# Three gated layers' last products in two-part float16, on one core of a Trainium2 chip

## The chip, the cores and the metric

The kernel runs on 1 NeuronCore of one Trainium2 chip. The number that counts is the device time of one execution in microseconds (us). The kernel before takes 786.88 us (median of 3 runs, 783.63 to 787.39). Engines are called as the profile calls them: PE is TensorE's matmul, PEld its weight load, DVE is VectorE, ACT is ScalarE, POOL is GpSimd, SP is SyncE.

## The reference, cut to what matters

Input is x of shape (2, 1024, 128); six layers are applied to it, each to the layer norm of x, each added back.

```python
x = x + 0.5 * int8_ffn(_layernorm(x))            # layer 0
x = x + attention_16_heads_of_8(_layernorm(x))   # layer 1, causal
x = x + 0.5 * int8_ffn(_layernorm(x))            # layer 2
x = x + 0.5 * gated_ffn(_layernorm(x))           # layer 3
x = x + attention_16_heads_of_64(_layernorm(x))  # layer 4, causal
x = x + 0.5 * gated_ffn(_layernorm(x))           # layer 5

def gated_ffn(x):                  # weights are integers in -127..127, times 1/127
    gate = x @ wg.T                # 128 -> 384
    up = x @ wu.T                  # 128 -> 384
    h = silu(gate) * up
    return h @ wd.T                # 384 -> 128
```

The gated layer is run four times: layer 3 and layer 5, each for batch 0 and batch 1. The change is about the last product, h @ wd.T, of three of the four.

## The kernel before, in words

Everything of one batch (1024 rows, 128 columns) is 8 tiles of 128 rows. A start section does the first layers of batch 0 by hand-written code. Then comes one list of 985 steps, `PLAN`, made from a string of letters, `ORDER`: each letter takes the next step of its own stream. Small letters are the attention of layer 1 in 8 groups of 4 heads (`m` maxima, `t` turning them, `e` exponentials, `w` weighing the values, `g` and `a` around them); capital letters are the attention of layer 4 in 16 pairs of heads (`Q`, `K`, `V` projections, `M` maxima, `T` turning them, `E` exponentials, `W` weighing, `S` sums, `O` output projection); `h` is the string of all the other layers, which depend on one another in order. Below, the stretch of the small letters is called the group stage and that of the capitals the pair stage. Every engine walks the same `PLAN` in the same order and does its part of each step, so a step that waits holds back all later steps on its engine. Behind the list a closing section finishes the last pair and runs layer 5 of batch 1 by hand-written code.

PE writes its products into PSUM. Steps that fill PSUM take banks in turn, two at a time for most (`deal_banks`), and PE waits until the readers of the earlier user of these banks are done (`wait_for_banks`). So some three such steps are under way at once.

A gated layer in the list is: the norm (`ln`, `xt`), six `up` steps (3 chunks of 128 hidden columns, 2 halves of 512 rows) and one `down` step. In an `up` step PE makes gate and up (float16 products, L1376), ACT takes the tanh of the gate (L808), and DVE makes h from them with two instructions (L1061, L1062), which go to `ffn_h` in float32. In the `down` step PE multiplies `ffn_h` by `wd_s`, 8 tiles by 3 chunks (24 matmuls in float32, L1382), and DVE adds the result to x (L1042).

POOL works in three roles here. In the start section it converts the weights of the gated layer (L570, L571) between other work (L580, L575) of the first attention. In the list it does most of the layer norms, the integer layer's rounding, and in the pair stage seven additions for each pair of heads: the exponentials of a chunk are added into a running sum (L679), 128x1024 elements each; and one multiplication (L525). ACT may not overwrite a chunk's buffer before PE has weighed it and POOL has added it; there are six such buffers.

A `T` step goes PE (L1444), ACT (L838), DVE (L1113), then two small DMAs on SP's queue into the tile that the first `E` step of the pair reads.

## Time and profile before

| | |
|---|---|
| median of 3 runs | 786.88 us (783.63 to 787.39) |
| the profiled execution's own time | 787.15 us |
| its span, first to last instruction | 785.4 us |
| busy over the span | PE 92%, PEld 55%, DVE 68%, ACT 58%, POOL 59% |
| mean granted PE clock | 0.963 of full |

The difference of 1.75 us between the profiled execution's time and its span lies before the first and behind the last instruction that the profile counts. Busy PE means that at least one matmul is in flight, so 92% is not 92% of PE's peak. An idle engine costs nothing unless the engine that sets the pace waits for it. The profile's rows stand in a section of their own below.

### The profile page before, as it was taken

To read this page: it belongs to the slowest core of one execution; us is meant where nothing else is said; L and a number is where in the kernel's file an instruction comes from. 1 tells how busy PE (TensorE), PEld (TensorE's weight loads), DVE (VectorE), ACT (ScalarE), POOL (GpSimd) and SP (SyncE) were. 2 spreads that over 40 slices of the span, in tenths; PEclk is the share of its full clock that TensorE was granted. 3 is DMA by queue.
4 is the path that set the end of the run, shared out by engine and by line. 5 is a ranking of instruction groups with operands and counts; after the bars stand their busy time and mean duration, and the time that the engine had idled before them with its cause. 6 is when DMAs were issued, how large, how long until landed. Compare 5 with 4: busy or idle time off the path is not lost.

```text
span 785.4 us, 21560 instructions
## 1 busy us (share of the span) xinstructions
PE 718.6 (92%) x9387; PEld 428.2 (55%) x9387; DVE 532.5 (68%) x730; ACT 454.4 (58%) x535; POOL 467.1 (59%) x367
## 2 busy tenths in 40 slices
PE   3667988889888899999999999999999999999997
PEld 1433535345344454655555566645776655557764
DVE  7599888998878785778587645665645655643037
ACT  2425876987776679554746546556544565563502
POOL 6814546522841210499989759978457967689630
PEclk9955998999889999999999999999999999999999
DMA  8000000000000000001001101110110110112100
...
DMA packets 13226, 16.20 MB, mean 21 GB/s; under 512 B 3053, under 2 KB 10573, under 8 KB 13133
## 3 DMA queue, kind: packets, MB, share of 16 engines
...
q8 instruction: 75, 1.23, 0.7%
...
## 4 chain that ended last, share of the span: by engine, by line
PE 74%; DVE 11%; ACT 9%; issue 3%; POOL 1%; DMA 1%; SPq 0%; ACTq 0%; DVEq 0%; POOLq 0%
PE ps L1261 20%; PE ps L1210 17%; ACT Pr L697 7%; DVE big L1074 7%; PE ps L1181 6%; PE ps L1425 5%; PE ps L1240 5%; PE ps L1464 3%; PE ps L1432 3%; PE ps L1382 2%; PE ps L1271 2%; PE ps L1376 2%; PE ps L1251 1%; PE ps L1221 1%; PE ps L1231 1%
## 5 line engine op out<-in xcount | busy, mean ns | idle before, releaser
L697 ACT ACTIVATE Pr<-ps,exp_scale 128x1024 f32<-128x1024 f32 (+1 forms) x294 | 278.8, 1006 | 122.2 <-PE ps L1261 74.1
L679 POOL TENSOR_TENSOR V0s<-V0s,Pr 128x1024 f32<-128x1024 f32 x77 | 181.4, 2356 | 106.4 <-PE ps L1210 60.6
L1105 DVE TENSOR_REDUCE mxb<-ps 128x8 f32<-128x1024 f32 (+1 forms) x152 | 173.6, 1163 | 86.0 <-PE ps L1261 66.5
L1074 DVE TENSOR_REDUCE big<-ps 128x8 f32<-128x1024 f32 (+1 forms) x159 | 170.2, 1116 | 22.7 <-PE ps L1240 16.0
L1261 PE MATMUL ps<-big 64*128 64x128 f16 (+2 forms) x2560 | 168.3, 259 | 0.9 <-DMA big<-turns 0.7
L1240 PE MATMUL ps<-big 32*128 32x128 f16 (+2 forms) x1280 | 105.1, 280 | 32.9 <-DVE big L1074 15.6
L1261 PEld LDWEIGHTS ps<-big 64*128 64x128 f16 x2560 | 92.8, 94 | 71.0 <-issue 23.9
L1210 PE MATMUL ps<-Pr,V1s 128*64 128x128 f32 (+2 forms) x960 | 110.2, 370 | 0.0
L1240 PEld LDWEIGHTS ps<-big 32*128 32x128 f16 x1280 | 42.5, 95 | 108.8 <-ACT Pr L697 44.0
L679 POOL TENSOR_TENSOR acts<-acts,Pr 128x1024 f32<-128x1024 f32 x35 | 82.4, 2355 | 22.3 <-PE ps L1210 12.4
L1210 PEld LDWEIGHTS ps<-Pr,V1s 128*64 128x64 f32 x960 | 57.0, 136 | 41.4 <-issue 28.2
L1181 PE MATMUL ps<-Pr,V0s 128*18 128x128 f32 (+2 forms) x1280 | 79.4, 373 | 0.2 <-ACT Pr L704 0.2
L1099 DVE TENSOR_TENSOR big<-ps,big 128x1024 f16<-128x1024 f32 (+1 forms) x33 | 39.0, 1191 | 30.3 <-ACT big L697 29.7
L1261 PE MATMUL ps<-big,shr_s 64*128 64x256 f16 (+2 forms) x384 | 55.8, 287 | 0.0
L1425 PE MATMUL ps<-XT,wqkv 128*128 128x512 f16 x192 | 45.2, 380 | 0.1
L697 ACT ACTIVATE big<-ps 128x1024 f16<-128x1024 f32 (+1 forms) x33 | 32.7, 997 | 19.8 <-PE ps L1425 19.7
L1181 PEld LDWEIGHTS ps<-Pr,V0s 128*18 128x18 f32 x1280 | 30.4, 100 | 18.8 <-issue 11.0
L594 POOL TENSOR_TENSOR stats<-moments 128x8 f32<-128x8 f32 x9 | 1.9, 210 | 63.1 <-DVE moments L1018 63.1
L525 POOL TENSOR_TENSOR big<-Pr,rec_b 128x1024 f32<-128x1024 f32 x15 | 36.5, 2431 | 3.7 <-DMA rec_b<-scratch_dram 2.5
L691 ACT ACTIVATE big<-ps 128x512 f32<-128x512 f32 (+2 forms) x31 | 19.3, 622 | 33.0 <-PE ps L1394 17.9
L697 ACT ACTIVATE V0s<-ps,exp_scale 128x1024 f32<-128x1024 f32 x22 | 24.5, 1114 | 19.1 <-PE ps L1251 17.8
L1425 PEld LDWEIGHTS ps<-XT,wqkv 128*128 128x128 f16 x192 | 17.4, 98 | 21.3 <-issue 2.1
...
## 6 DMA issues: line engine op xcount, KB each, us to landing
...
```

Source lines behind the costliest of these rows:

```text
L525: g.tensor_tensor(YT[:, p % NP], y_raw[p % 2], rec_b[:], ALU.mult).then_inc(normed, 1)
L679: g.tensor_tensor(dst, dst, src, ALU.add).then_inc(summed, 1)
L697: ins = a.activation(dst[:, part], src, func, scale=scale)
L1074: ins = v.tensor_reduce(maxima_of(mall[:, r, 2 * u:2 * u + 2][:, part], i), block_view(src, i), AX.X, ALU.max, negate=True)
L1099: ins = v.tensor_tensor(in_banks(low)[:, part], src, in_banks(high)[:, part], ALU.subtract)
L1105: ins = v.tensor_reduce(maxima_of(mxb[:, r][:, part], arg), block_view(src, arg), AX.X, ALU.max, negate=True)
L1181: ins = te.matmul(ps[HR * j:HR * j + 2 * VW, ACC0, a0 - 512 * half:a1 - 512 * half], values(g // GB, t, GH * (g % GB) + j, half), src, sta ...
L1210: ins = te.matmul(ps[h * D1:(h + 1) * D1, ACC1[bank], a0 - 512 * bank:a1 - 512 * bank], V1[p % SETS][:, t, h * D1:(h + 1) * D1], src, star ...
L1240: ins = te.matmul(slot[h][:, off:off + a1 - a0], still[rows, tile(t)], moving[rows, a0:a1], start=q == 0, stop=cut is None and q == len(pi ...
L1261: ins = te.matmul(slot[h][:, off:off + a1 - a0], still[rows], moving[rows], start=q == 0 and k == 0, stop=not goes_on and q == len(pieces) ...
L1425: ins = te.matmul(slot[half], w16[:, ww], x16[:, xx, half_of(half)], start=part == 0, stop=part == 2)
L1432: ins = te.matmul(tile_of(slot, t), x16[:, xx, tile(t)], w16[:, ww], start=part == 0 and t % 4 == 0, stop=part == 2, skip_group_check=True)
```

## The change

Three of the four gated layers are touched: layer 3 of both batches, and layer 5 of batch 0, the ones in the list. Layer 5 of batch 1, in the closing section, keeps its float32 product.

- A new kind of step, `split`, stands behind each `up` step, six in a layer. DVE now writes h of an `up` step into one of three buffers (`ffn_t`, float32). In the `split` step ACT copies it to float16 (the high part), and POOL subtracts the high part from h and writes the remainder in float16 (the low part). DVE waits before it writes a buffer again until POOL has read it.
- `down` multiplies both parts by a float16 copy of the integer weights (`wd_16`), 8 tiles by 3 chunks by 2 parts: 48 matmuls in float16 in place of 24 in float32.
- The up weights, and with them h, are scaled by 2^-14 (`H_SCALE`); the scale factors behind are set for it. In the start section POOL's one conversion of gate and up weights becomes two instructions, and the copy to `wd_16` is added at the end of POOL's start work.
- `ORDER` is another string: 1003 steps in place of 985, with all letters placed anew.
- The program's scratch for dynamic DMA is set to 1024.

```diff
 def gated_steps(s, b):
-    return (turned_norm_steps(s, b) + [("up", (s, b), (c, half), "AV") for c in range(HC) for half in range(2)]
-            + [("down", (s, b), None, "V")])
+    ups = [[("up", (s, b), (c, half), "AV"), ("split", (s, b), 2 * c + half, "")] for c in range(HC) for half in range(2)]
+    woven = ups[0][:1] + [step for k in range(1, len(ups)) for step in (ups[k][0], ups[k - 1][1])] + ups[-1][1:]
+    return turned_norm_steps(s, b) + woven + [("down", (s, b), None, "V")]
...
-    "ammmmmmmmammmmmmmmmmamtmmehemehmhmemememmmweehmwemmwemwemewemehwmehewemhthweaemehweemwegemehwmemwemm"
+    "ammmmmmmmammmmmmmmmmamtmmmeeehemmhhememmmwmhewemewemewemhwmemwememehemwthweahemeweehmwegemehwmemwmem"
...
+        ffn_t = sb("ffn_t", [P, TERMS, 512])
+        ffn_16 = ffn_h[:, :, :].rearrange("p c s -> p (c s)").bitcast(F16).rearrange("p (w c s) -> p w c s", w=2, c=HC)
...
             pool.wait_ge(raw_in, 16 * R_LOADS)
-            g.tensor_copy(wg_s[:], raw_gu)
+            g.tensor_copy(wg_s[:, 0], raw_gu[:, 0])
+            g.tensor_scalar(wg_s[:, 1], raw_gu[:, 1], H_SCALE, None, ALU.mult)
             g.tensor_scalar(wd_s[:], raw_d, W_SCALE, None, ALU.mult).then_inc(converted, 1)
...
+            g.tensor_copy(wd_16[:], raw_d).then_inc(converted, 1)
...
+                if kind == "split":
+                    c, half = divmod(arg, 2)
+                    pool.wait_ge(h_high, SPLIT_NO[key, arg] + 1)
+                    g.tensor_tensor(ffn_16[:, 1, c, half_of(half)], ffn_t[:, arg % TERMS], ffn_16[:, 0, c, half_of(half)],
+                                    ALU.subtract).then_inc(h_low, 1)
...
+                if kind == "split":
+                    c, half = divmod(arg, 2)
+                    act.wait_ge(slot_dve, read("V", "up", key, (c, half)))
+                    a.activation(ffn_16[:, 0, c, half_of(half)], ffn_t[:, arg % TERMS], ACT.Copy).then_inc(h_high, 1)
...
-                    v.tensor_tensor(ffn_h[:, c, 512 * half:512 * half + 512], gate, slot[1],
-                                    ALU.mult).then_inc(slot_dve, 1)
+                    if 2 * c + half >= TERMS:
+                        dve.wait_ge(h_low, SPLIT_NO[key, 2 * c + half - TERMS] + 1)
+                    v.tensor_tensor(ffn_t[:, (2 * c + half) % TERMS], gate, slot[1], ALU.mult).then_inc(slot_dve, 1)
...
                 if kind == "down":
-                    pe.wait_ge(slot_dve, read("V", "up", key, (HC - 1, 1)))
+                    pe.wait_ge(h_low, SPLIT_NO[key, GATED - 1] + 1)
+                    pe.wait_ge(converted, 2)
                     for t in range(T):
                         for h in range(HC):
-                            ins = te.matmul(tile_of(slot, t), ffn_h[:, h, tile(t)], wd_s[:, h], start=h == 0,
-                                            stop=h == HC - 1)
+                            for w in range(2):
+                                ins = te.matmul(tile_of(slot, t), ffn_16[:, w, h, tile(t)], wd_16[:, h],
+                                                start=(h, w) == (0, 0), stop=(h, w) == (HC - 1, 1))
...
-    nc = bacc.Bacc("TRN2", target_bir_lowering=False, num_devices=1)
+    nc = bacc.Bacc("TRN2", target_bir_lowering=False, num_devices=1, dynamic_dma_scratch_size=1024)
```

What the new code and the new string do to the engines' instructions is shown at three places. In the first, POOL in the start section, before and after; `wg_s` and `wd_s` are the converted weights, `V1s` and `big` belong to the first attention's keys and queries.

```order
L568 MEMSET big 128x512
L570 CAST wg_s<-Pr 128x768
L571 TENSOR_SCALAR wd_s<-Pr 128x384
L580 TENSOR_TENSOR big<-V1s,big 128x8x8x8
L575 TENSOR_TENSOR V1s<-V1s,big 128x1024
```

```order
L578 MEMSET big 128x512
L580 CAST wg_s<-Pr 128x384
L581 TENSOR_SCALAR wg_s<-Pr 128x384
L582 TENSOR_SCALAR wd_s<-Pr 128x384
L591 TENSOR_TENSOR big<-V1s,big 128x8x8x8
L586 TENSOR_TENSOR V1s<-V1s,big 128x1024
```

One TENSOR_SCALAR more stands ahead of the first subtraction for keys and queries (L580 before, L591 after).

The second place is POOL after the change, during layer 3 of batch 1 in the pair stage. L696 are the additions of exponentials (L679 before), L535 the multiplication (L525 before), L675 the new subtractions of the `split` steps.

```order
L696 TENSOR_TENSOR acts<-acts,Pr 128x2x512
L675 TENSOR_TENSOR ffn_h<-ffn_t,ffn_h 128x512
L696 TENSOR_TENSOR acts<-acts,Pr 128x8x128
L696 TENSOR_TENSOR acts<-acts,Pr 128x2x512
L535 TENSOR_TENSOR big<-Pr,rec_b 128x1024
L696 TENSOR_TENSOR V0s<-V0s,Pr 128x2x512
L696 TENSOR_TENSOR V0s<-V0s,Pr 128x4x256
L696 TENSOR_TENSOR V0s<-V0s,Pr 128x2x512
L675 TENSOR_TENSOR ffn_h<-ffn_t,ffn_h 128x512
L696 TENSOR_TENSOR V0s<-V0s,Pr 128x4x256
```

The subtractions stand one by one between the additions; before, nothing of the gated layer's products stood on POOL.

The third place is PE at the last `down` step of the list (layer 5, batch 0), before and after. L1382 and L1407 are `down`, L1444 and L1469 the `T` step of the last pair, L1432 its `V` step, L1210 and L1233 `W` steps, L1261 and L1284 (128x128 x24) the first of its `E` steps.

```order
L1221 MATMUL ps<-pick_s,cutq_s 128x4x64 x4
L1382 MATMUL ps<-wd_s,ffn_h 128x128 x24
L1444 MATMUL ps<-id_s,mxc 16x128
L1432 MATMUL ps<-wqkv,XT 128x128 x24
L1210 MATMUL ps<-Pr,V1s 64x512 x2
L1210 MATMUL ps<-Pr,V1s 64x128 x16
L1261 MATMUL ps<-big 128x128 x24
```

```order
L1244 MATMUL ps<-pick_s,cutq_s 128x4x64 x4
L1233 MATMUL ps<-Pr,V1s 64x256 x4
L1233 MATMUL ps<-Pr,V1s 64x512 x2
L1233 MATMUL ps<-Pr,V1s 64x128 x8
L1469 MATMUL ps<-id_s,mxc 16x128
L1407 MATMUL ps<-wd,ffn_h 128x128 x48
L1233 MATMUL ps<-Pr,V1s 64x128 x8
L1284 MATMUL ps<-big 128x128 x24
```

Before, `down` stood ahead of the `T` step, and the `V` step and three `W` steps between `T` and `E`; now `down` and one `W` step stand between them.

## Rows read from the trace of the kernel before

**Rows 1.** Windows of the four stages: us; busy of each engine (instructions); PEclk, DMA.
```profile
0.00:34.80 34.80, 15.51 (x93) 10.42 (x93) 24.94 (x65) 9.03 (x21) 25.50 (x58) 1.00 0.48 156
34.80:321.40 286.60, 246.76 (x3639) 131.68 (x3639) 237.75 (x319) 206.60 (x250) 102.44 (x116) 0.90 0.01 2
321.40:742.00 420.60, 419.71 (x5366) 259.35 (x5365) 248.48 (x290) 232.37 (x258) 328.73 (x190) 1.00 0.08 21
742.00:785.40 43.40, 36.67 (x295) 26.76 (x294) 21.32 (x57) 6.37 (x11) 10.39 (x5) 1.00 0.09 25
```

**Rows 2.** Page, section 2: PE's granted clock in 40 slices, tenths of full.
```profile
PEclk9955998999889999999999999999999999999999
```

**Rows 3.** Timeline, first `down`: start, us, engine, line, out<-in, count, [idle before <-releaser].
```profile
256.73 5.43 PEld L1382 LDWEIGHTS ps<-wd_s,ffn_h 128*128 128x128 f32 x48 [0.23 <-issue]
...
262.40 1.23 DVE L1042 SCALAR_TENSOR_TENSOR X<-ps,X 128x1024 f32<-128x1024 f32 x1 [3.49 <-PE ps L1382]
...
262.78 3.28 ACT L697 ACTIVATE Pr<-ps,exp_scale 128x512 f32<-128x512 f32 x4 [5.93 <-PE ps L1240]
```

**Rows 4.** Timeline, one `V` step's weight loads.
```profile
318.74 1.34 PEld L1432 LDWEIGHTS ps<-wqkv,XT 128*128 128x128 f16 x24
```

**Rows 5.** Groups by form: count, busy us, mean ns, idle before and releasers.
```profile
L1382 PEld LDWEIGHTS ps<-wd_s,ffn_h 128*128 128x128 f32 x144 | 16.3, 192 | 0.9 <-issue 0.9
L1062 DVE TENSOR_TENSOR ffn_h<-ffn_g,ps 128x512 f32<-128x512 f32 x18 | 12.4, 687 | 0.6
L1061 DVE SCALAR_TENSOR_TENSOR ffn_g<-ffn_g,ps 128x512 f32<-128x512 f32 x18 | 12.3, 684 | 14.3 <-ACT ffn_g L808 14.3
L658 POOL TENSOR_TENSOR big<-V1s,big 128x512 f16<-128x512 f32 x4 | 4.5, 1156 | 2.9 <-ACT big L796 2.9
L796 ACT ACTIVATE big<-V1s 128x512 f16<-128x512 f32 x4 | 2.3, 636 | 1.3 <-POOL V1s L652 1.3
```

**Rows 6.** Windows, POOL alone, 330 to 470 us: busy, PEclk, DMA.
```profile
330.00:470.00 140.00, 118.97 (x77) 1.00 0.07 18
```

**Rows 7.** Waits, 330 to 470 us: us in total, times, longest.
```profile
POOL V0s L679 <- POOL V0s L679: 3.0, 18, 0.2
```

**Rows 8.** Timeline, 29.9 to 36 us.
```profile
29.97 0.82 POOL L570 CAST wg_s<-Pr 128x768 f16<-128x768 int32 x1
30.52 1.34 DVE L997 TENSOR_TENSOR V1s<-V1s,big 128x1024 f32<-128x1024 f32 x1
30.76 2.15 POOL L571 TENSOR_SCALAR wd_s<-Pr 128x384 f32<-128x384 int32 x1
31.97 1.15 ACT L739 ACTIVATE big<-V1s 128x512 f16<-128x512 f32 x2 [7.55 <-DVE V1s L997]
33.15 0.69 DVE L989 TENSOR_TENSOR big<-V1s,big 128x512 f16<-128x512 f32 x1
33.20 1.66 POOL L580 TENSOR_TENSOR big<-V1s,big 128x512 f16<-128x512 f32 x1 [0.28 <-ACT big L739]
33.76 1.28 DVE L993 TENSOR_TENSOR big<-ps,big 128x512 f32<-128x512 f32 x2
35.09 0.90 PEld L1394 LDWEIGHTS ps<-idh_s,big 128*128 128x128 f16 x16 [4.02 <-DVE big L993]
```

**Rows 9.** Line L580 alone: shortest, median, longest in ns.
```profile
L580 POOL TENSOR_TENSOR big<-V1s,big x3: 1152/1158/1658, 33.2 to 39.8; 128x512 f16<-128x512 f32 x3
```

**Rows 10.** Timeline, the last pair's `T` to its first `E`.
```profile
720.45 0.27 PE L1444 MATMUL ps<-id_s,mxc 128*16 128x128 f32 x1
...
720.65 1.29 DVE L1042 SCALAR_TENSOR_TENSOR X<-ps,X 128x512 f32<-128x512 f32 x2 [3.32 <-PE ps L1382]
...
725.55 0.85 PE L1261 MATMUL ps<-big 64*128 64x128 f16 x24 [0.73 <-DMA big<-turns]
```

**Rows 11.** Windows, two stretches at a lower clock.
```profile
120.10:127.00 6.90, 5.41 (x48) 4.31 (x41) 5.22 (x6) 2.83 (x6) 5.12 (x4) 0.61 0.02 6
208.80:219.10 10.30, 8.53 (x91) 4.38 (x91) 7.43 (x8) 4.55 (x6) 6.31 (x5) 0.58 0.01 3
```

More of the change, by code:

```diff
@@ L120, in summed_columns @@
     return view[:, :, :, a % every:a % every + z - a]
+GATED = 2 * HC
+TERMS = 3
+H_SCALE = 2.0**-14
 GROUP_BUFS = 6
@@ L185 @@
 ORDER = (
-    "ammmmmmmmammmmmmmmmmamtmmehemehmhmemememmmweehmwemmwemwemewemehwmehewemhthweaemehweemwegemehwmemwemm"
-    "emwemwmehmewmmhmemhmewmeemetmmhmhmwhhmmhmememwmeegemwememhhwmmehhhewemwaemwememwhemmhetmwemememwmeme"
-    "mwmeewmememwemamewemewemetmemwemwemewmegemehwmemwmegeamhmmhehewewemmemhhwemewehmhewemmewemmemtwemmam"
-    "mwheehwemmewheehwemewememewmhemwememewemheegthhhwhhhwememwmmheewmemheewemewhmeewmememwmemwemwemhweme"
-    "mQQtKKVgeeMwMeVMeweMeweMeweMewMeeweMgewMeeweeTKQwwMMgEVEMWMEMWMEMWMEEhMEMhEMWhEMWTKQWWWMEMhWhMEEMWWh"
-    "MEEMSMWWMEMWMEEEMWMTQhMKWWWMEMVSMEEMWEMMWWWMEEEWMEEhTKQhWWWWMEEEhVWhhMEMWMEWMEMWMMSWTEMEWMEEQKhWWMMW"
-    "EMhhWEMWTEMMWEEMWhVhShWWMEEEhQWWEMMWEMEWKTEWWMEhhVSEMEWhMMMWWWMEEEWWMEEMWMEEEEhWWWWQVKTVSMEEMWWEMMWW"
-    "MEMWMEEEEQKWWMEEMSMEMWTMWWWMMKQWWMEEEEWWEMMWWEMSMEMWTEMWMEMWWMEMWMEEMVQKVOSMMOMEEEMWWWWMEEEKQTOOhVME"
-    "WWWhMMMWWMETSMEEEEMWWWWMEEEMWEMQVKhWWWMMWMEMWTSMEEEEEMWWMEEEWMMQVKMMWWWWhhWEEEEEMWMMMWWWMEWMSEThWWEM"
-    "WMEWMEEhKVWEMhQTWWWMEEEhWESEMEWWWWMEEEMWWSMEMWWMEEEEWWMMhTVWWWEEEEWWWOSEEEEEOOOWWWWWW"
+    "ammmmmmmmammmmmmmmmmamtmmmeeehemmhhememmmwmhewemewemewemhwmemwememehemwthweahemeweehmwegemwemehmwmem"
+    "emwemwemhmewmmhmemmewhmeeemhmwmmhmmtmhhhmememwmeehmegewemmwhmhehwmemheweamewemmtewemewmemwemeemwmeme"
+    "mwemmeamewemewmewemmemhwemewmemwetmememwhmegemmweehgamhmmheewwehhemmwhmewhememehmwemewmemwetmemmweme"
+    "mamhmehweemheweehwemwemwmeemewmememwmehhewtehhhhhhhhhhhwemehmwmemgehemwemheewhemewemewmeemewmemwemwm"
+    "mhewmmQKQtVVMegeeMweMeweMeweMeweMeweMeweMeweeMweegKTQKwwMMgEEEWWMEMWMMEWEMhMEEMhTVMEWhWWEMMWhWhEMEWM"
+    "EMWMMKhVQhWWMEEEMWSMWMEMWTEMhWMMEWEMVhQKMWWEMEhEEhESWTMEMWMMWWMEEMWMhKQWWMEESTVEMMWWMEEEEMWhWWEMQhWE"
+    "MWMhhhKWWMEEMWhMEMWMEEVhhhTWWSMMWEEEWMhEhKQWWWhhMEEEMWEMMWhThSEhEEWWWWMEEMWWWMEEEEMWWWMMhWWMMKQVTSME"
+    "EEEWMEMWMMKQWWMEEMWMEMEEMTSMWMEEMWWMEMWWWMMQKVWWMEMEEMWWMEEEEWTSWWWMEEMWEMKVQVWWMEEEEMWWMOOTMOEMEWMM"
+    "OSMEEEMWhWVQKWMhMWWWEMEMMWWMETSEEMWWMEEEEMWhQMWWWWMEEEVhhKWWMESMWTMEEMWWhWEMEWWMEMWMEEEEhhhMWWWMEESQ"
+    "TKWWWMEhEEMWWMMQhVWEMMhWWMEEEEEMWWSMEEWWTVKVhWhMWMEMhWMEEMWWMEEEESEMWWWMEMWWWThWEEEEWWWOOSEEEEEOOWWW"
+    "WWW"
 )
@@ L201 @@
 READS = {e: list(accumulate(int(e in step[3]) for step in PLAN)) for e in "AV"}
+SPLIT_NO = {step[1:3]: n for n, step in enumerate([step for step in PLAN if step[0] == "split"])}
 NORM_NO = {step[1]: n for n, step in enumerate([step for step in PLAN if step[0] == "ln" and step[2] == 0])}
@@ L291, in macaron_block_kernel @@
         wd_s = sb("wd_s", [P, HC, P])
+        wd_16 = sb("wd_16", [P, HC, P], F16)
         id_s = sb("id_s", [P, P])
@@ L1041, in _ @@
                         at = in_banks(X[:, b].rearrange("p t c -> p (t c)"))[:, part]
-                        ins = v.scalar_tensor_tensor(at, src, 1.0 if kind == "wo0" else 0.25 * W_SCALE**2, at, ALU.mult, ALU.add)
+                        ins = v.scalar_tensor_tensor(at, src, 1.0 if kind == "wo0" else 0.25 * W_SCALE**3 / H_SCALE, at,
+                                                     ALU.mult, ALU.add)
                     ins.then_inc(slot_dve, 1)
@@ L1163, in _ @@
                 dve.wait_ge(last_down, half + 1)
-                v.scalar_tensor_tensor(at, bank(1 + half).rearrange("p (t c) -> p t c", t=4), 0.25 * W_SCALE**2, at,
+                v.scalar_tensor_tensor(at, bank(1 + half).rearrange("p (t c) -> p t c", t=4), 0.25 * W_SCALE**2 / H_SCALE, at,
                                        ALU.mult, ALU.add).then_inc(last_x, 1)
```

1 line of the change is left out of this document (added).

## The prediction

> **What bounds the kernel now.** I read the windows by stage first. In the pair stage, 321.4 to 742 us, PE is busy 419.71 of 420.60 us, at the full clock, while DVE, ACT and POOL have 92 to 188 us to spare [rows 1]. Whatever leaves PE there comes off the time, unless another engine then becomes late. In the group stage, 34.8 to 321.4 us, PE is busy 246.76 and DVE 237.75 of 286.60 us and the granted clock is 0.90 [rows 1]: no engine alone sets the pace, the matmuls and their readers take turns. The start and the last 43.4 us are chains of single waits; the change leaves the last section's work as it is. The clock row shows the half-speed stretches, all before the pair stage [rows 2].
>
> **The change part by part.**
>
> The product. A `down` step has 24 float32 matmuls in the code and 48 weight loads in the trace, so one float32 matmul counts as two. The first of the three `down` steps loads for 5.43 us [rows 3]; with one load taking 0.192 us [rows 5] that is (5.43 − 0.19)/47 = 0.111 us from one to the next. The float16 price is in the `V` steps, which have the same form (128x128 weights, 128 columns, new weights each time): 24 matmuls in the code, 24 in the trace, 1.34 us [rows 4], with a load of 0.10 us (0.098 in the trace's group) (1.34 − 0.10)/23 = 0.054 us each. The new `down` has 48 such, 0.10 + 47 × 0.054 = 2.64 us. It saves 5.43 − 2.64 = 2.8 us, three times 8.4 us. The bounds are 0, if the float16 products went at 0.111 us, and 8.4; I take 8.4 since the `V` row has the very shape.
>
> Where it counts. In the pair stage PE has no idle time, so two layers give 5.6 us. In the group stage the first `down` holds everybody: DVE sat idle 3.49 us and ACT 5.93 us until it and the next scores were done [rows 3]. So its 2.8 us lie on the path too; next late would be DVE, which had 3.49 us of idle there and keeps 0.7.
>
> The added steps. ACT gets 18 copies of 128x512 to float16; L796 is such a copy, 0.636 us [rows 5], so 3.8 us a layer. POOL gets 18 subtractions; L658 has exactly their form, 1.156 us [rows 5], and a gap of 3.0/18 = 0.17 us between dependent additions [rows 7], so 6 × 1.33 = 8.0 us a layer. Behind PE's full pair stage ACT's cost is covered: ACT is busy 232 of 421 us [rows 1].
>
> In the group stage the six `up` steps are DVE's: 6 × (0.684 + 0.687) = 8.2 us [rows 5]. The new wait of DVE for the third buffer back asks for a copy and a subtraction, 0.64 + 1.16 = 1.8 us and handovers, inside three `up` steps of 1.37 = 4.1 us, so DVE does not stand, and with it neither the maxima queued behind it nor their PSUM banks. Behind the sixth product, though, copy and subtraction come in sequence before `down`, 1.8 us, and ACT's exponentials are queued behind the copies. The new string puts two `e` steps, three `m`, a `w` and a `g` step in between on PE, so part is covered. Between 0 and 3.8 us (all of ACT's copies) I take 1.2.
>
> POOL in the pair stage. Between 330 and 470 us POOL is busy 118.97 of 140 us [rows 6]. Of the 21.0 us idle, 3.0 are the gaps between additions [rows 7]; 18.0 are left. Layer 3 of batch 1 puts 8.0 us more there, and the stretch gets 2.8 us shorter: 10.8, so 7 us are still free. The subtractions also stand singly between the additions, as the order shows, so none makes an addition wait long behind it; a chunk's buffer comes round after six chunks. I take 0, with 16 us (all 12 subtractions of the pair stage) as the other end.
>
> The start. Before, POOL works without a pause through L570 and L571 until 32.91, and starts L580 at 33.20, when ACT's copy is there; L580 ends at 34.86, DVE's L993 at 35.04, and PE's first transposes for the groups wait for both and begin at 35.09 [rows 8]. After, a conversion of half the size (0.41 for 0.82) and one more TENSOR_SCALAR of 128x384 stand there. L571 took 2.15 us for that size, but while it ran DVE's L997 (two operands in SBUF, 1.34 us) ran too; and L580, which takes 1.15 us alone, took 1.66 beside L989, also with two [rows 8, 9]. So I read L571 as 0.8 us of work and 1.34 of standing still. Then POOL is later by 0.8 − 0.4 = 0.4 us, of which 0.28 + 0.18 us are slack. If the 2.15 were all work, it would be 2.15 − 0.41 = 1.74 late, and PE 1.3. I take 0.4, between 0 and 1.3.
>
> The Trainium skill says so of this stretch: GPSIMD Engine Reference, section Key points, has GpSimd share its SBUF interfaces with VectorE, with contention beside VectorE instructions "with two SBUF inputs". The trace agrees: 1.66 beside L989 against a shortest of 1.152 us [rows 8, 9]. By that rule the start costs 0.4 us or less; without it the bare row gives 1.3, and the sum 0.9 more. It also speaks for 1.16 us as a split's price, because DVE's gated products read one operand from PSUM.
>
> The string. Everything moves by a few steps. One place is plain: before, the last `T` (720.45) waited on DVE behind the `down` of the step before (1.29 us), and PE stood 0.73 us until the shift row had landed, 5.1 us after `T` [rows 10]. After, `T` comes ahead of `down`, and what lies between is 2.64 us of `down` and one `W` step. That takes the 1.29 us out of the chain and leaves 3.8, of which `down` covers 2.64 and the `W` step most of the rest: up to 0.7 gained. At the third pair the new string leaves only one `E`, one `W`, three `M` and one small step between `T` and the first `E`, and about as much may be lost again. I take 0 for the string, between −3 and +3 us, an estimate from the 0.9 us that PE stands in the whole pair stage and the 40 us in the group stage [rows 1].
>
> The sum, against the profiled execution's 787.15 us: 787.15 − 5.6 − 2.8 + 1.2 + 0.4 + 0 = 780.35 us. The profiled one lies 0.27 above the median of the runs, 786.88, so I predict 780.3.
>
> **The rivals.**
>
> *The group stage keeps its gain.* There DVE is busy 83% and ACT 72% [rows 1]; if the next late engine takes over at once, 2.8 us are hidden, and 787.15 − 5.6 + 1.2 + 0.4 = 783.2, with the 1.3 us of the start 784.1. For it speaks the mixed bound; against it, DVE's and ACT's long idle time at the very place.
>
> *GpSimd sets the pace (slower).* The price is the 12 subtractions of the pair stage, 16.0 us, on the path: 780.35 + 16.0 = 796.3. It works so: a subtraction waits for ACT's copy and holds the additions behind it; ACT's exponentials then wait for their buffers, DVE for its third buffer, and PE for both, and `down` for the last subtraction. It decides once more than 6.8 of the 16 us fall on the path (780.35 + 6.8 = 787.15). For it: POOL is at 85% between 330 and 470 us [rows 6]. Against it: 7 us of room there, and PE waits nowhere there now.
>
> *The clock moves.* Two short stretches at 0.61 and 0.58 cost at most half of PE's busy time in them, (5.41 + 8.53)/2 = 7.0 us [rows 11]. If both go, 773.3; another like the longer adds 4.3, 784.6. In TensorE: Matmul & The Clock Gate, section The HAM clock gate, the Trainium skill has the clock set by how busy PE has been of late; the change makes PE a little less busy in the group stage, so by it a further dip is likelier than one fewer. In the trace both dips lie in the stage where PE is not full, 246.76 of 286.60 us [rows 1], which agrees.
>
> *The products are no faster.* At 0.111 us each the layer saves nothing: 787.15 + 1.6 = 788.8. The `V` rows are against it.
>
> **How the numbers follow.** Forecast 0.60 (own range 777 to 783); group stage hidden 0.17; GpSimd 0.09; clock, both dips gone, 0.07, one more 0.04; products no faster 0.03. The range leaves out most of the GpSimd case and half of the dips gone: 775.0 to 785.8. Half a per cent, about what a measurement of this kernel can tell, is 3.9 us, so the bounds are 782.9 and 790.8. Faster: 0.93 of the forecast, 0.07 of the clock and a third of the hidden case, 0.68. Slower: the GpSimd case and a little, 0.09. Same: 0.23.
>
> **What would show it.** `down` should stand with 48 float16 loads in 2.6 us, three times; 5.0 to 6.5 us should be gone from the pair stage with PE still full. PE's first transposes should begin at 35.1 to 35.5 us, the TENSOR_SCALARs of POOL at 0.8 us where DVE's L997 is not beside them. The new subtractions should take 1.16 us and no engine should list a wait for them over 1 us. The prediction is wrong if PE idles more than 2 us in the pair stage, if a long wait of `down` or of DVE for the subtractions stands in the waits, or if the group stage ends later than 320 us at the same clock.

## The result, and the profile after

The changed kernel takes 775.13 us (median of 4 runs, 773.71 to 777.87), the kernel before 785.25 us in the same comparison (4 runs, 783.05 to 787.39). The ratio is 0.9876, with an interval of 0.9837 to 0.9915: faster by 1.2% (0.8 to 1.6%). A second comparison (e0_after below) gives 0.9863 [0.9842, 0.9885]. The forecast was 780.3 us with a range of 775.0 to 785.8: the median lies 0.13 us inside the lower end of the range, and below the 777 to 783 us that the forecast case itself was given. Two executions of the kernel before in the later comparisons took 1711.9 us, more than twice the others, and are left out of every number here.

The profiled execution took 773.71 us, 13.4 less than the 787.15 of before. The windows of the four stages say where they went; columns as in [rows 1].

```profile
0.00:34.90 34.90, 17.49 (x93) 12.61 (x93) 25.24 (x65) 9.41 (x22) 25.85 (x59) 0.90 0.48 155
34.90:313.20 278.30, 239.51 (x3620) 126.66 (x3621) 237.82 (x319) 208.00 (x250) 109.96 (x123) 0.93 0.01 2
313.20:728.50 415.30, 415.11 (x5363) 254.97 (x5361) 249.87 (x291) 234.05 (x261) 339.29 (x201) 1.00 0.08 22
728.50:771.90 43.40, 36.75 (x322) 26.71 (x316) 20.97 (x57) 9.42 (x14) 12.98 (x6) 1.00 0.09 25
```

Against [rows 1] the start is 0.1 us longer, the group stage 8.3 shorter (286.6 to 278.3), the pair stage 5.3 shorter (420.6 to 415.3) with PE as full as before, the end the same. The sum had 0.4 us, 1.6 us, 5.6 us and nothing for these four; 6.7 us of the group stage's gain are not in it.

The clock row, which answers to [rows 2]:

```profile
PEclk9855999999999999999999999999999999999999
```

Slices 7, 11 and 12, which read 8 before, read 9 now; slice 2 reads 8 for 9, and the first transposes came 0.1 us later. The windows of before's two short half-speed stretches [rows 11], with some more around them, in before:

```profile
119.00:130.00 11.00, 9.05 (x113) 6.85 (x114) 8.21 (x11) 6.13 (x10) 6.22 (x4) 0.69 0.02 4
208.00:222.00 14.00, 11.89 (x159) 6.63 (x155) 10.35 (x11) 5.86 (x8) 7.11 (x5) 0.63 0.01 2
```

and in the changed kernel:

```profile
119.00:130.00 11.00, 10.08 (x128) 6.73 (x118) 9.85 (x11) 6.26 (x11) 5.31 (x4) 0.84 0.02 4
208.00:222.00 14.00, 11.10 (x235) 7.35 (x231) 12.77 (x19) 11.01 (x15) 7.04 (x4) 1.00 0.01 4
```

The longer stretch is gone (granted clock 1.00 for 0.63) and the other is half as long.

The new operations, from the groups by form (count | busy us in total, mean ns of one | idle time of the engine before them, and what ended it), answering to [rows 5]:

```profile
L1407 PEld LDWEIGHTS ps<-wd,ffn_h 128*128 128x128 f16 x144 | 8.1, 98 | 1.3 <-ACT Pr L714 1.3
L675 POOL TENSOR_TENSOR ffn_h<-ffn_t,ffn_h 128x512 f16<-128x512 f32 x18 | 20.7, 1157 | 14.5 <-ACT ffn_h L829 14.5
L829 ACT ACTIVATE ffn_h<-ffn_t 128x512 f16<-128x512 f32 x18 | 11.2, 628 | 1.5 <-DVE ffn_t L1086 1.5
L1086 DVE TENSOR_TENSOR ffn_t<-ffn_g,ps 128x512 f32<-128x512 f32 x18 | 12.4, 687 | 0.6
```

The weight loads took 16.3 us before and take 8.1; a subtraction takes 1.157 us, a copy 0.628. POOL's 14.5 us of idle ahead of the subtractions hold nobody up: DVE's L1086, which waits for them, has 0.6 us of idle in all.

The first `down`, answering to [rows 3] (timeline of 251 to 256 us):

```profile
250.65 1.16 POOL L675 TENSOR_TENSOR ffn_h<-ffn_t,ffn_h 128x512 f16<-128x512 f32 x1 [1.95 <-ACT ffn_h L829]
...
252.24 2.68 PEld L1407 LDWEIGHTS ps<-wd,ffn_h 128*128 128x128 f16 x48 [0.45 <-ACT Pr L714]
...
252.56 1.13 ACT L714 ACTIVATE Pr<-ps,exp_scale 128x1024 f32<-128x1024 f32 x1
...
255.14 1.29 DVE L1063 SCALAR_TENSOR_TENSOR X<-ps,X 128x512 f32<-128x512 f32 x2 [1.58 <-PE ps L1407]
255.52 1.11 ACT L714 ACTIVATE Pr<-ps,exp_scale 128x1024 f32<-128x1024 f32 x1 [1.84 <-PE ps L1263]
```

2.68 us in place of 5.43. The last subtraction ends at 251.81, 0.4 us ahead of it; ACT idles 1.84 us where it idled 5.93, DVE 1.58 where it idled 3.49.

The start section, answering to [rows 8]:

```profile
29.82 0.50 POOL L580 CAST wg_s<-Pr 128x384 f16<-128x384 int32 x1
30.37 1.23 DVE L1018 TENSOR_TENSOR V1s<-V1s,big 128x1024 f32<-128x1024 f32 x1
30.39 2.26 POOL L581 TENSOR_SCALAR wg_s<-Pr 128x384 f16<-128x384 int32 x1
...
32.71 1.18 POOL L582 TENSOR_SCALAR wd_s<-Pr 128x384 f32<-128x384 int32 x1
...
32.88 0.88 DVE L1010 TENSOR_TENSOR big<-V1s,big 128x512 f16<-128x512 f32 x1
...
33.85 1.16 POOL L591 TENSOR_TENSOR big<-V1s,big 128x512 f16<-128x512 f32 x1
...
35.23 1.05 PE L1419 MATMUL ps<-idh_s,big 128*128 128x128 f16 x16 [1.91 <-POOL big L591]
```

The first transposes begin at 35.2 us (35.1 before). The first of two TENSOR_SCALARs of one shape takes 2.26 us; DVE's addition of two SBUF operands (1.23 us) had begun 0.02 us ahead of it. The second takes 1.18 us, although 0.88 us of such an instruction, begun 0.17 us behind it, runs beside it. In e3, e5, e6 and e8 (see below) that instruction of DVE begins 0.37 to 0.40 us behind the second TENSOR_SCALAR and takes 0.68 us, and the TENSOR_SCALAR takes 1.18 to 1.19 again, so 1.18 us is its undisturbed length; if it is the first one's too, that one stood still for 1.1 of DVE's 1.23 us. The long ones are those that begin behind DVE's instruction: 2.26 us here, 2.15 (L571) and 1.66 (L580) in [rows 8]. That the order of the two starts decides is read from these rows; no run swaps it for one pair. L591, which begins when DVE's instruction has ended, takes 1.16 us where L580 had taken 1.66. The direction is that of the Trainium skill (GPSIMD Engine Reference, section Key points); the size isn't told by it.

The last `T` to its first `E`, answering to [rows 10]:

```profile
707.97 0.28 PE L1469 MATMUL ps<-id_s,mxc 128*16 128x128 f32 x1
...
708.08 2.84 PE L1407 MATMUL ps<-wd,ffn_h 128*128 128x128 f16 x48
...
712.13 0.85 PE L1284 MATMUL ps<-big 64*128 64x128 f16 x24 [0.18 <-DMA big<-turns]
```

4.2 us for 5.1, and 0.18 us of waiting for 0.73.

### The profile page after: what moved, and what is told of

Same layout as the page of the kernel before. It is cut to its first block, busy times and chain, and to the rows that moved or that the text cites. A ratio compares the mean times of both kernels' runs of the same rounds, so it can differ in the third digit from the quotient of the medians.

```text
span 771.9 us, 21579 instructions
## 1 busy us (share of the span) xinstructions
PE 708.9 (92%) x9387; PEld 421.0 (55%) x9387; DVE 533.9 (69%) x730; ACT 460.9 (60%) x544; POOL 488.1 (63%) x387
## 3 DMA queue, kind: packets, MB, share of 16 engines
q8 instruction: 75, 1.23, 0.7%
## 4 chain that ended last, share of the span: by engine, by line
PE 73%; DVE 11%; ACT 8%; issue 3%; POOL 3%; DMA 1%; SPq 0%; ACTq 0%; DVEq 0%; POOLq 0%
PE ps L1284 21%; PE ps L1233 17%; DVE big L1097 7%; ACT Pr L714 6%; PE ps L1204 6%; PE ps L1263 6%; PE ps L1450 6%; PE ps L1489 3%; PE ps L1457 3%; PE ps L1294 2%; PE ps L1399 2%; PE ps L1274 1%; PE ps L1244 1%; PE ps L1407 1%; PE ps L1254 1%
## 5 line engine op out<-in xcount | busy, mean ns | idle before, releaser
L696 POOL TENSOR_TENSOR V0s<-V0s,Pr 128x1024 f32<-128x1024 f32 x77 | 181.4, 2356 | 94.4 <-PE ps L1233 58.7
L1284 PE MATMUL ps<-big 64*128 64x128 f16 (+2 forms) x2560 | 169.2, 260 | 0.7 <-ACT Pr L714 0.4
L1284 PEld LDWEIGHTS ps<-big 64*128 64x128 f16 x2560 | 93.3, 94 | 73.7 <-issue 23.6
L1233 PE MATMUL ps<-Pr,V1s 128*64 128x128 f32 (+2 forms) x960 | 110.5, 371 | 0.0
L696 POOL TENSOR_TENSOR acts<-acts,Pr 128x1024 f32<-128x1024 f32 x35 | 83.2, 2378 | 18.7 <-PE ps L1233 8.4
L1204 PE MATMUL ps<-Pr,V0s 128*18 128x128 f32 (+2 forms) x1280 | 77.8, 368 | 0.2 <-ACT Pr L721 0.2
L1233 PEld LDWEIGHTS ps<-Pr,V1s 128*64 128x64 f32 x960 | 56.2, 137 | 37.8 <-issue 21.4
L1284 PE MATMUL ps<-big,shr_s 64*128 64x256 f16 (+2 forms) x384 | 56.0, 287 | 0.0
L1122 DVE TENSOR_TENSOR big<-ps,big 128x1024 f16<-128x1024 f32 (+1 forms) x34 | 39.3, 1160 | 18.9 <-ACT big L714 18.2
L535 POOL TENSOR_TENSOR big<-Pr,rec_b 128x1024 f32<-128x1024 f32 x15 | 35.5, 2369 | 0.7 <-POOL acts L696 0.7
L675 POOL TENSOR_TENSOR ffn_h<-ffn_t,ffn_h 128x512 f16<-128x512 f32 x18 | 20.7, 1157 | 14.5 <-ACT ffn_h L829 14.5
```

Source lines behind the costliest of these rows:

```text
L535: g.tensor_tensor(YT[:, p % NP], y_raw[p % 2], rec_b[:], ALU.mult).then_inc(normed, 1)
L696: g.tensor_tensor(dst, dst, src, ALU.add).then_inc(summed, 1)
L1122: ins = v.tensor_tensor(in_banks(low)[:, part], src, in_banks(high)[:, part], ALU.subtract)
L1204: ins = te.matmul(ps[HR * j:HR * j + 2 * VW, ACC0, a0 - 512 * half:a1 - 512 * half], values(g // GB, t, GH * (g % GB) + j, half), src, sta ...
L1233: ins = te.matmul(ps[h * D1:(h + 1) * D1, ACC1[bank], a0 - 512 * bank:a1 - 512 * bank], V1[p % SETS][:, t, h * D1:(h + 1) * D1], src, star ...
L1284: ins = te.matmul(slot[h][:, off:off + a1 - a0], still[rows], moving[rows], start=q == 0 and k == 0, stop=not goes_on and q == len(pieces) ...
```

## The experiments

For each kernel the table gives when four steps of PE begin, in us of its profiled execution: the first group transposes, the turning of group 6's maxima (a `t` step; groups count from 0), the first `W` step, and the last `W` step of the list. Two profiles of one kernel (after and e0_after) differ by 1 us in them, nearly all of it ahead of the first turn (60.3 and 61.3). Kernels whose steps are the same up to group 6 differ by more: from the first transposes to group 6 it is 202.4, 203.3, 204.9 and 204.6 us in after, e0_after, e3 and e6, and 209.2, 210.0, 207.6 and 207.6 us in before, e1, e5 and e8. So single profiles can't tell less than some 2.5 us there; behind group 6 the profiles of after, e0_after, e7 and e9 agree within 0.1 us up to the first `W` and within 0.5 us from there to the last. The runs e0 to e3 were measured beside the kernel before on one chip, e4 to e7 on a second, e8 and e9 on a third; across these, ratios are the fairer measure.

| kernel | first transposes | group 6 | first W | last W | span |
|---|---|---|---|---|---|
| before | 35.1 | 244.3 | 321.4 | 752.9 | 785.4 |
| after | 35.2 | 237.6 | 313.2 | 739.5 | 771.9 |
| e0_after | 35.1 | 238.4 | 314.0 | 740.5 | 773.0 |
| e1_old_string | 35.2 | 245.2 | 321.4 | 752.2 | 784.7 |
| e2_new_string_f32 | 34.9 | 237.4 | 315.8 | 747.5 | 780.0 |
| e3_f32_group_layer | 35.2 | 240.1 | 318.5 | 745.3 | 777.8 |
| e4_old_keep | 36.0 | 242.3 | 319.3 | 750.8 | 783.3 |
| e5_late_splits | 35.1 | 242.7 | 318.4 | 747.2 | 779.7 |
| e6_split_twice | 35.3 | 239.9 | 321.3 | 748.7 | 781.2 |
| e7_new_keep | 35.5 | 238.5 | 314.2 | 740.2 | 772.7 |
| e8_ups_moved | 35.2 | 242.8 | 318.6 | 746.2 | 778.7 |
| e9_new_keep_late | 35.2 | 239.8 | 315.5 | 742.0 | 774.5 |

Below, "the pair part" is the time from the first `W` to the last `W`: 431.5 us before, 426.3 after.

**e0_after: the changed kernel again.** No edit.

> The changed kernel again, beside the three others on one chip, as their measure. Both theories: ratio to the kernel before 0.985 to 0.991. Theory A (products): PE's saved 8.4 us make nearly all of the gain. Theory B (string): the new string of steps gives 3 to 5 us by itself in the group stage. The runs of this one also tell how far a run's time goes with the length of its half-speed stretches.

Measured: 775.96 us (5 runs, 774.49 to 776.71), ratio 0.9863 [0.9842, 0.9885]. The gain stands.

**e2_new_string_f32: the new string alone.** The kernel before, with the string of the change less its 18 split letters:

```
 ORDER = (
-    "ammmmmmmmammmmmmmmmmamtmmehemehmhmemememm...
+    "ammmmmmmmammmmmmmmmmamtmmmeeehemm...       (the new one, without the splits)
```

> The kernel before (float32 products, no split steps) in the new string of steps with the split letters taken out. Theory A: 0 to 2 us from before, ratio 0.998 to 1.002. Theory B: 3 to 5 us less, ratio 0.993 to 0.996, with the group stage shorter by that and the pair stage as before.

Measured: 784.20 us, ratio 0.9963 [0.9946, 0.9979], at the upper edge of theory B. The string alone gives 0.4% (0.2 to 0.5%), so the rest, 0.9863 for 0.9963, belongs to the products: 1.0%, 7.9 us. (This rest also holds the scratch setting and the conversions at the start; no run has these alone.) In the trace the string's gain is all in the group stage: the first `W` comes 5.6 us earlier, the pair part is 431.7 us for 431.5. This profile is one of the fastest of its 12 runs (781.78 us), so its 5.6 us are more than the median's 2.9. And e0_after against e2: pair part 5.2 us shorter (two layers, 5.6 forecast); from group 6 to the first `W` 75.6 us for 78.4, 2.8 shorter.

**e3_f32_group_layer: the changed kernel, with layer 3 of batch 0 as before.**

```
+WIDE = (3, 0)
-                if kind == "split":
+                if kind == "split" and key != WIDE:      (ACT and POOL)
+                if kind == "down" and key == WIDE:       (24 products of ffn_h and wd_s in float32)
```

> The changed kernel with the one gated layer that lies in the group stage (layer 3, batch 0) back in float32, without its six ACT copies and POOL subtractions. If that layer's saving lies on the path there, as the prediction has it, it is 1.6 us slower than the changed kernel (2.8 less 1.2 for the copies). If the group stage hides it, 0 to 0.5 us.

Measured: 779.68 us, ratio 0.991 [0.9889, 0.9932]. From group 6 to the first `W` it takes 78.4 us where the changed kernel takes 75.6: the layer in the group stage is worth its whole 2.8 us. The copies and subtractions ahead of `down` cost nothing there: from group 6 to `down` it is 14.7 us with them and without. The pair part is 426.8 us. By the medians the kernel is 3.7 us slower than e0_after, more than the 1.6 expected; in the profile another 1.7 us lie ahead of group 6 (240.1 for 238.4), where the steps are the same.

**e1_old_string: the products alone.** The changed code in the old string, with the split letters put in right behind the up letters. Layer 3 of batch 1 in letters (u is an up step, s a split, D the down; a dot is one other step, (13) are thirteen):

```
 before  u u (13) u . u . u (6) u (18) D
 e1      u u s (13) u s . u s . u s (6) u s s (18) D
```

> The two-part float16 products in the string of steps of before; the new split steps are put directly behind the up steps (split k-1 behind up k, the last two behind the last up), nothing else moves. Theory A: the products alone give 5.6 us in the pair stage and 1.6 to 2.8 in the group stage, so 6.5 to 8.5 us less than before, ratio 0.989 to 0.992. Theory B: 2 to 6 us less, ratio 0.993 to 0.997, the rest of the gain being the string's. If the string had to be placed anew for the splits, PE shows waits for POOL or DVE around down, and the ratio is over 0.997.

Measured: 784.21 us, ratio 0.9981 [0.996, 1.0003]. This is neither theory A nor B but the third case, a ratio over 0.997 with PE waiting for POOL or DVE: products that are worth 1.0% in the new string are worth 0.2% in the old one, and the interval reaches to nothing. Each `down` still is 2.8 us shorter; but ahead of the three, 1.2, 2.3 and 2.6 us have come in (counted from group 6, from the first `W`, and from the `down` before it). Behind the first `down` the clock also fell once more: from 260 to 270 us it is 0.83, and 1.00 before. The timeline around layer 3 of batch 1 shows how (start, length, engine, line, [idle before, releaser]):

```profile
440.56 2.37 POOL L696 TENSOR_TENSOR V0s<-V0s,Pr 128x1024 f32<-128x1024 f32 x1 [0.17 <-POOL V0s L696]
...
442.89 3.39 POOL L675 TENSOR_TENSOR ffn_h<-ffn_t,ffn_h 128x512 f16<-128x512 f32 x3
444.16 0.69 DVE L1086 TENSOR_TENSOR ffn_t<-ffn_g,ps 128x512 f32<-128x512 f32 x1 [1.87 <-POOL ffn_h L675]
...
444.99 0.34 PE L1284 MATMUL ps<-big 64*128 64x128 f16 x6 [1.00 <-DVE ffn_t L1086]
...
453.26 0.40 PE L1284 MATMUL ps<-big 64*128 64x128 f16 x8 [0.77 <-DVE big L1122]
```

Three subtractions stand behind POOL's queue of additions and run in one piece; DVE waits 1.87 us for its third buffer and PE 1.00 us for DVE. In the group stage, where ACT's copies stand ahead of its exponentials, PE's timeline has:

```profile
255.30 0.40 PE L1263 MATMUL ps<-big 32*128 32x128 f16 x8 [0.70 <-DVE ffn_t L1086]
257.03 0.39 PE L1263 MATMUL ps<-big 32*128 32x512 f16 x2 [1.11 <-ACT Pr L714]
```

and ahead of the last `down` PE waits for a sum that stands on POOL behind an addition and two subtractions:

```profile
706.30 1.07 PE L1294 MATMUL ps<-V0s,ones_s 128*32 128x512 f32 x8 [1.26 <-POOL V0s L696]
```

**e5_late_splits: the same, the splits later.** Only the string: each split some steps behind its up step.

```
 e1      u u s (13) u s . u s . u s (6) u s s (18) D
 e5      u u (7) s (6) u . s u . s u (6) s u (5) s (7) s (6) D
```

> The float16 products in the old string once more, but each split a few steps behind its up step (in the pair stage 7 to 9 steps where the next up step leaves room, the last one 12 and 18 steps behind; in the group stage the last two 3 and 6 steps behind) instead of right behind it. Theory A (the old string gave its gain back because the splits stood right behind the ups and held the exponentials of ACT and the additions of POOL): the waits of 1 to 2 us ahead of the two down steps of the pair stage are gone, PE's stretch from the first weigh to the last pair is 426 to 428 us as with the new string, and the ratio to before is 0.989 to 0.993. Theory B (the new placing of the ups and of all other steps is what makes room, not the distance of the splits): the stretch stays at 430 us or more and the ratio at 0.996 to 0.999 as with the splits right behind.

Measured: 782.56 us, ratio 0.9953 [0.9926, 0.9979]. Part of the gain over e1 in the ratio may be clock: this profile has no half-speed stretch at 210 us, where e1's has one. The times behind group 6 are free of that stretch. From group 6 to the first `W` it is 75.7 us (77.1 before, 76.2 in e1): half of that layer's 2.8 us. The other half is a wait of PE for the last subtraction:

```profile
256.58 2.84 PE L1407 MATMUL ps<-wd,ffn_h 128*128 128x128 f16 x48 [1.56 <-POOL ffn_h L675]
```

The pair part is 428.8 us, between what the two theories expected (426 to 428, and 430 or more). The last `down` gives its full 2.7 us (first `W` to it 393.7 us, before 393.6); layer 3 of batch 1 gives next to nothing, since first `W` to `down` is 142.6 us for before's 140.0. Two waits of PE stand there, in the table of waits of 418 to 462 us (in total, times, longest):

```profile
PE ps L1407 <- ACT Pr L714: 1.4, 1, 1.4
PE ps L1284 <- DVE ffn_t L1086: 0.8, 1, 0.8
```

The second is DVE waiting for its third buffer again (1.5 us, for a subtraction): three up steps stand within 4 us and their subtractions meet the additions.

**e8_ups_moved: the ups of that layer moved too.**

```
 e5      u u (7) s (6) u . s u . s u (6) s u (5) s (7) s (6) D
 e8      u u s u (3) s (8) u s u (12) s . u (5) s s (10) D
```

> The kernel e5_late_splits with one more edit: in layer 3 of batch 1 the up steps are moved too, to the distances from the down step that they have in the new string (at the 0th, 0th, 0th, 11th, 11th and 24th of the 39 other steps in place of the 0th, 0th, 13th, 14th, 15th and 21st), and the splits at the 0th, 3rd, 11th, 23rd, 29th and 29th. Theory A (in that layer three ups within 4 us meet POOL's queue of additions, DVE waits 1.5 us for its third buffer, and this ate the 2.8 us of its down step; with the ups apart the wait goes): PE's stretch from the first weigh to the last pair falls from 428.8 to 426 to 427 us, and the time is 2 to 3 us below that of e5_late_splits (782.56 median): 779.5 to 780.5, ratio to before 0.990 to 0.994. Theory B (the loss sits in what surrounds the down step itself, in the old order of exponentials and weighings there): the stretch stays within 0.7 us of 428.8 and the time within 1 us of 782.56.

Measured: 780.53 us, ratio 0.9942 [0.9916, 0.9968]. That is 2.0 us less than e5_late_splits' 782.56 in the medians, but on another chip; the ratios, 0.9953 and 0.9942, are not told apart by their intervals. What shows the effect is the profile: the pair part, 427.6 us, is 1.2 shorter, more than the 0.7 of theory B, though it misses theory A's 426 to 427. DVE has no wait for a subtraction there any more, and of PE's waits in 418 to 461 us one is left:

```profile
PE ps L1284 <- ACT acts L714: 1.0, 1, 1.0
```

So with these moves the old string gives most of what the products are worth: the pair part is 3.9 us shorter than before, and from group 6 to the first `W` it is 75.8 us for 77.1, 5.2 of 8.4 us together. Of the other 3 us 1.56 are PE's wait for the last subtraction at the first `down`, which stands here as in e5, and 1.0 may be the wait in the row above; this is read from the timeline, no run takes either away.

**e6_split_twice: how much room POOL has.**

```
+                    for again in range(2):
+                        ins = g.tensor_tensor(ffn_16[:, 1, ...], ffn_t[:, ...], ffn_16[:, 0, ...], ALU.subtract)
+                        ...                     (the first releases the second, the second counts h_low up)
```

> The changed kernel with each of the 18 subtractions on POOL done twice, the second waiting for the first: 1.3 us more of POOL per split, 8 us more in each layer. Theory A (POOL has room left: 18 us idle of 140 in its fullest stretch before, 8 of them used by the change): another 8 us fit just, down waits for its last subtraction by 0.5 us or less each time, and the time is 0 to 3 us above the changed kernel's 775.5 (ratio to before 0.986 to 0.990). Theory B (POOL is at its limit already): every added microsecond in the pair stage shows, 8 to 16 us more, ratio 0.997 or above.

Measured: 782.86 us, ratio 0.9957 [0.9935, 0.998], 6.9 us above e0_after: outside both expectations (it is another chip's median; the ratios say 0.9%), as it falls into two parts. In the pair part, with 16 us more on POOL, 427.4 us for 426.5: hidden but for 0.9. In the group stage, with 8 us more, group 6 to the first `W` takes 81.4 us for 75.6, 5.8 more. There the six subtractions follow one another behind the ups, and twice their length is more than what stands beside them: POOL's twelve take 14.1 us without a pause, `down` begins when they end, and it is 4.2 us farther from group 6 than in the changed kernel (18.9 for 14.7). DVE waits for its buffers (waits of 240 to 262 us):

```profile
DVE ffn_t L1091 <- POOL ffn_h L676: 2.1, 2, 1.1
```

Another 1.5 us are clock. PE waits 1.07 us for DVE until 250.3 us and 1.68 us for ACT until 252.6 us; from about 251 us the clock is at half speed for some 10 us, and `down` lies in that stretch, 4.36 us of PE for 2.85 (a window, and the timeline):

```profile
251.00:262.00 11.00, 9.45 (x107) 7.08 (x108) 6.16 (x8) 5.17 (x7) 7.46 (x7) 0.54 0.01 1
258.80 4.36 PE L1412 MATMUL ps<-wd,ffn_h 128*128 128x128 f16 x48
```

The changed kernel is at full clock there.

In the fullest stretch of POOL, which answers to [rows 6], it is now busy 128.23 of 140 us, and 123.92 in the changed kernel:

```profile
330.00:470.00 140.00, 128.23 (x88) 1.00 0.07 18
```

**e4_old_keep: the clock alone.** The kernel before with 22 matmuls more, whose results are overwritten, ahead of its two short half-speed stretches:

```
+    ('gexp', 1, (8, 0)): 2, ('gmax', 3, (0, 0)): 3, ('gexp', 1, (8, 1)): 1,
+    ('gmax', 6, (0, 1)): 1, ('gexp', 4, (7, 0)): 2, ('gexp', 4, (7, 1)): 3, ('gmax', 6, (1, 0)): 3,
+    ('gexp', 4, (8, 0)): 2, ('gexp', 4, (8, 1)): 2, ('gmax', 6, (2, 1)): 3,
```

> The kernel before with 22 further matmuls of the shape 128x512 (0.23 us each at full clock, results overwritten) in the places where PE idled just ahead of its two short half-speed stretches (3 steps near 119 us, 7 steps between 205 and 216 us). Everything else is as before. Theory A (the new string is faster because the clock does not fall at 210 us any more): both stretches are gone, the granted clock between 205 and 225 us reads 0.95 or more, and the layer after the groups starts 2 to 5 us earlier than 321.4 us, so the ratio to before is 0.994 to 0.998. Theory B (the clock is a bystander; the new string is faster by the order of its steps): the stretches may be gone, but the start of the pair stage stays within 1 us of 321.4, or comes later by the 2 to 4 us that the further matmuls take; ratio 1.000 to 1.005.

Measured: 785.08 us, ratio 1.0 [0.9975, 1.0026]. Both stretches are at full clock now:

```profile
119.00:130.00 11.00, 10.05 (x140) 6.65 (x139) 10.19 (x12) 6.79 (x10) 6.72 (x4) 1.00 0.02 4
208.00:222.00 14.00, 12.20 (x208) 6.72 (x207) 9.92 (x14) 7.44 (x9) 5.89 (x4) 1.00 0.01 4
```

and the time from the first transposes to the first `W` is 283.3 us for 286.3, 3.0 less, with the further matmuls paid for. The medians don't show it, and the runs of before suggest why: their mean granted clock comes at two values for the most part. In the three comparisons on one chip each, the 15 runs of before at 0.969 took 783.6 us in the mean, the 27 at 0.960 or 0.961 took 787.6. (The profiled one had 0.963 and 787.15.) A reading that fits is that the longer stretch is in some executions and not in others. No profile of before without it was taken, but e5 and e8 run before's steps up to 244 us, and in their profiles it is not there; a short one (176 to 180 us) is:

```profile
208.00:222.00 14.00, 10.80 (x214) 6.66 (x218) 12.25 (x16) 8.41 (x11) 8.38 (x8) 1.00 0.01 2
```

This row is e5's. From the first transposes to group 6 these two take 207.6 us, before and e1, which have the longer stretch, 209.2 and 210.0. So it costs 1.6 to 2.4 us more than the short one by the profiles; the 4 us between the two values of before can hold more than this one stretch. Nine of e4's 11 runs lie between 784.4 and 785.8: it trades the two values of before for one in the middle, for 22 × 0.23 = 5.1 us of further matmuls, some of them where PE idled. By the profile I had to choose theory A, by the median theory B; both are right about what they measure.

**e7_new_keep: the long half-speed stretch.** The changed kernel with 52 such matmuls in groups 0 and 1.

```
+    ('gmax', 0, (1, 0)): 2, ... ('gmax', 0, (8, 1)): 2, ('gmax', 1, (0, 0)): 2, ... ('gmax', 1, (1, 1)): 2,
+    ('gexp', 0, (0, 0)): 1, ... ('gexp', 0, (2, 1)): 1, ('gmax', 1, (2, 0)): 1, ... ('gmax', 1, (4, 1)): 1,
```

> The changed kernel with 52 further matmuls of 128x512 (results overwritten) in the maxima and exponentials of groups 0 and 1, between 38 and 72 us, where PE ran at half speed for 37 us while DVE was busy all the time. Theory A (DVE sets the pace of the maxima there, but from 58 us on the turn between PE, ACT and DVE is longer at half speed): the clock comes back earlier than 75 us, gturn of group 1 starts 1 to 2 us earlier than 89.0, ratio to before 0.984 to 0.987. Theory B (DVE hides the half speed wholly): no gain, the further matmuls delay the maxima by up to 3 us, ratio 0.987 to 0.991.

Measured: 774.90 us, ratio 0.9867 [0.9828, 0.9906]. The mean clock of the run is 0.991, and this stretch has 0.92 where the changed kernel has 0.54. First the changed kernel, then e7:

```profile
34.90:76.00 41.10, 28.97 (x301) 14.57 (x301) 37.52 (x48) 16.94 (x27) 15.42 (x23) 0.54 0.01 2
```

```profile
34.90:76.00 41.10, 35.84 (x349) 14.90 (x353) 36.51 (x47) 16.77 (x28) 14.18 (x23) 0.92 0.01 2
```

DVE gets no more done, and the step of group 1 that turns its maxima starts at 89.9 us as in e0_after (89.8); theory A had it 1 to 2 us earlier. So giving the clock back brought nothing that can be told where DVE is busy nine tenths of the time, though the further matmuls (52 × 0.23 = 12 us of PE) may have eaten a small gain.

**e9_new_keep_late: the short stretch that is left.** The changed kernel with 9 such matmuls, at 118 to 120 and 201 to 202 us.

```
+    ('gexp', 1, (8, 1)): 2, ('gmax', 3, (0, 0)): 1, ('gmax', 3, (0, 1)): 2,
+    ('gmax', 5, (8, 0)): 3, ('gexp', 4, (5, 1)): 1,
```

> The changed kernel with 9 further matmuls of 128x512 (results overwritten), 5 of them at 118 to 120 us, ahead of its short half-speed stretch, and 4 at 201 to 202 us, where PE idles 0.9 us. If the remaining short stretch costs what the two of the kernel before did, about 1.5 us for 3.4 us at half speed, and the dummies cost 0.23 us each where PE is needed and nothing where it idles: 0 to 1.5 us faster than the changed kernel, 774 to 775.5, ratio to before 0.984 to 0.987. If the order of the turns sets the pace there and the clock is hidden: no change or up to 2 us slower, 775.5 to 777.5.

Measured: 775.31 us, ratio 0.9847 [0.9817, 0.9877]: no difference from the changed kernel that can be told. No version tried is clearly better than the changed kernel.

## Why the prediction was right, and where it was not

**The products.** Forecast 2.8 us for each of the three. Measured 5.2 to 5.4 us for the two in the pair stage (426.3 and 426.5 against 431.7) and 2.8 for the one in the group stage (e3). The durations were right too: 2.68 us of loads, 2.64 forecast. The `V` steps were the right rows to take.

**The added steps in the group stage.** Forecast +1.2, between 0 and 3.8; measured 0. The steps that the new string puts between the sixth up and `down` cover all of copy and subtraction. This term was mis-sized, and e6 says how much room is behind it: of 8 us more of subtraction 4.2 show up to `down`, so somewhat under 4 us is there.

**POOL in the pair stage.** Forecast 0, with 7 us of room; that held. With 8 us more in that layer PE lost 0.9 us in the whole stage. The rival in which GpSimd sets the pace was fairly priced as unlikely for this string. But the reason given was half of it: I argued from POOL's free time over 140 us. e1 has the same sum of POOL's work and lost 4.5 of the 5.2 us in the pair stage. What decides is where the subtractions and the up steps stand: moving the subtractions alone (e5) gave back 2.0 of the 4.5 us, moving one layer's up steps with them (e8) another 1.2, and 1.3 stay open.

**The start.** Forecast +0.4, measured +0.1 (35.2 for 35.1), in its bounds, but not by its working. It had POOL 0.4 us late with 0.28 + 0.18 us of slack, which would have cost nothing, and still took 0.4. The TENSOR_SCALAR that came in was priced at 0.8 us and takes 1.18: L571's 2.15 us less all 1.34 of DVE's took off too much, since DVE's instruction had begun 0.24 us ahead of L571. What made up for it was not forecast: L591 no longer ran beside DVE's instruction, 1.16 us for 1.66.

**The string.** The step that failed is "I take 0 for the string, between −3 and +3 us". Measured alone it is −5.6 us in the profiled execution and 0.37% (2.9 us) in the comparison. Where I looked, it was near the forecast: at the last pair PE's wait fell from 0.73 to 0.18 us, up to 0.7 expected; the third pair lost nothing (6.3 us from `T` to `E` before, 3.5 now, and PE waits for nothing there). But I took both ends from PE's idle time at single places and looked at the clock only as a rival by itself. The clock was part of the string: e4 puts it at about 3.0 us of the 5.6 in the profile, which would leave 2.6 for the order of the steps. That is an estimate, not a measured split: e4 removes both stretches where the new string keeps half of one, and its further matmuls cost time of their own. The runs at the highest clock of each kernel point the same way: before at 0.969 took 783.6 us in the mean, the new string alone at 0.971 took 781.8 (4 runs), 1.8 less; the changed kernel at 0.969 to 0.971 took 774.3 (4 runs), 7.5 less again, near the 6.8 us forecast for all but the string. Which moves in the order make the rest was not tested.

**The clock rival.** It put 7.0 us on both stretches; removing them gave 3.0 in e4's profile. Half of PE's busy time was an upper end, since the other engines' work runs beside it. It was given 0.07, and the longer stretch did go. I read the Trainium skill (TensorE: Matmul & The Clock Gate, section The HAM clock gate) as speaking for a further dip, since PE is less busy in the stage as a whole. The trace went the other way, and the page's rule need not be wrong for it: in e4's profile 16 further matmuls between 205 and 216 us took the longer stretch away, and in e6 a half-speed stretch came in among waits of PE of 1.07 and 1.68 us. But the steps alone don't settle it, since before's steps have the stretch in one profile (before, e1) and not in another (e5, e8).

**The sum.** With the measured terms: 787.15 − 5.3 − 2.8 + 0 + 0.1 − 5.6 = 773.55 for the profiled 773.71. The string's 5.6 is from a fast execution, as the profiled one of the changed kernel is, so the good agreement is in part luck. Against the profiled execution the sum's 780.35 missed by 6.6 us, of which the string is 5.6 and the added steps 1.2. (A slip in it: 0.27 below 780.35 is 780.1, not the 780.3 that was forecast.) Against the medians it missed by 5.2 us, and there the string is 2.9. That the change is faster, and by its products, was forecast; that 775.13 still fell into the range was close, by 0.13 us, and owed to a bound drawn for another case, the clock's.

One assumption was never written as a step: that terms add up. String and products don't. The products bring 0.2% in the old string and 1.0% in the new one, so in a sum of "products 8.4, string 0" the string was doing more than its own row says: it made room for the splits. e5 and e8 show some of the moves that do it.
